# A Fourier tower's mixing written out with three buffers, and its inverse with half input tiles and two group buffers

## The reference, cut to what matters

```python
def _spectral_conv(h, w1, w2):
    xf = jnp.fft.rfft2(h)
    top = jnp.einsum('bixy,ioxy->boxy', xf[:, :, :M1, :M2], w1)
    bot = jnp.einsum('bixy,ioxy->boxy', xf[:, :, -M1:, :M2], w2)
    ...
    return jnp.fft.irfft2(of, s=(h.shape[-2], h.shape[-1]))
for l in range(LAYERS):
    sc = _spectral_conv(h, w1r[l] + 1j * w1i[l], w2r[l] + 1j * w2i[l])
    pw = jnp.einsum('bihw,oi->bohw', h, pw_w[l]) + pw_b[l][None, :, None, None]
    y = sc + pw
    ...
    h = jax.nn.gelu(y, approximate=False)
```

## Time and profile before

| | us |
|---|---|
| median of 3 runs | 5555.8 (5553.83 to 5564.04) |
| the profiled execution | 5561.11 |
| its span, first to last instruction | 5559.3 |

### The profile page before, as it was taken

How to read it: one execution, slowest core, us unless ns; L and a number is a source line. 1 busy time by engine, 2 the same in 40 slices (tenths; PEclk the granted TensorE clock), 3 DMA queues, 4 the chain that set the end, 5 groups by cost and what they waited for, 6 DMA issues and landing times. The chain is left out here.

```text
span 5559.3 us, 115640 instructions
## 1 busy us (share of the span) xinstructions
PE 3813.1 (69%) x50724; PEld 2545.1 (46%) x50724; DVE 2993.7 (54%) x3933; ACT 2535.4 (46%) x1968; POOL 56.9 (1%) x51
## 2 busy tenths in 40 slices
PE   5676885657666656576667566766678994668677
PEld 4354773435455534354555344545552223623532
DVE  1437987853666678536666784366660003344344
ACT  0112335521677755116777451167778991112122
POOL 0000000000000000000000000000000001000000
PEclk9888997888888878888889788888899995579579
DMA  1654656755677667556776675567765431000000
GB/s 34 253 215 172 224 219 258 288 213 226 243 288 289 268 253 289 219 211 257 289 289 257 264 281 224 207 257 288 288 258 206 170 123 36 0 0 1 0 0 8
DMA packets 184510, 1093.16 MB, mean 197 GB/s; under 512 B 20613, under 2 KB 92517, under 8 KB 122465
## 3 DMA queue, kind: packets, MB, share of 16 engines
q1 hardware_dynamic: 160578, 802.32, 37.6%
q10 hardware_dynamic: 22592, 285.22, 13.3%
q0 software_dynamic: 1024, 1.05, 0.1%
HBM read 683.80 MB, written 404.75 MB: 196 GB/s over the span
## 5 line engine op out<-in xcount | busy, mean ns | idle before, releaser
L509 PE MATMUL bank<-arena 128*64 128x128 f32 x16384 | 1130.4, 295 | 161.2 <-ACT arena L552 142.4
L509 PEld LDWEIGHTS bank<-arena 128*64 128x64 f32 x16384 | 1080.0, 221 | 314.0 <-issue 313.9
L587 DVE STREAM_TRANSPOSE arena<-bank 64x512 f32<-64x512 f32 x1024 | 731.4, 714 | 388.2 <-PE bank L485 357.3
L552 ACT ACTIVATE arena<-bank,pwb 128x1024 f32<-128x1024 f32 x512 | 567.0, 1108 | 608.0 <-PE bank L509 603.8
L543 ACT ACTIVATE arena<-arena,shift,scale 64x2048 f32<-64x2048 f32 x384 | 803.0, 2091 | 71.1 <-ACT arena L552 39.4
L361 PE MATMUL bank<-arena 128*32 128x128 f32 x8192 | 596.0, 476 | 309.0 <-DVE arena L388 309.0
L595 DVE BATCH_NORM_STATS2 stats<-arena 128x6 f32<-128x512 f32 x1024 | 634.0, 672 | 228.3 <-ACT arena L552 228.2
L361 PEld LDWEIGHTS bank<-arena 128*32 128x32 f32 x8192 | 423.4, 142 | 481.5 <-issue 327.6
L485 PE MATMUL bank<-arena,ga 64*64 64x512 f32 x2048 | 309.5, 728 | 476.2 <-DMA arena<-spec_out 420.8
L728 ACT ACTIVATE arena<-arena,shift,scale 128x1024 f32<-128x1024 f32 x384 | 445.1, 1230 | 404.5 <-DMA arena<-y_dram 404.3
L688 PE MATMUL bank<-arena,fwq 32*32 32x512 f32 x6144 | 316.9, 842 | 350.5 <-DVE arena L733 350.5
(11 more groups left out here) (208 smaller groups left out, 2845.5 us busy)
## 6 DMA issues: line engine op xcount, KB each, us to landing
arena<-y_dram SPq DMA_DIRECT2D x224, 2048.0 KB, 8.5
y_dram<-arena ACTq DMA_DIRECT2D x128, 2048.0 KB, 8.0
arena<-spec_in SPq DMA_DIRECT2D x32, 2048.0 KB, 8.9
arena<-in_w_modes SPq DMA_DIRECT2D x32, 2048.0 KB, 13.3
spec_out<-arena SPq DMA_DIRECT2D x64, 1024.0 KB, 3.9
arena<-spec_out SPq DMA_DIRECT2D x32, 2048.0 KB, 21.0
spec_in<-arena SPq DMA_DIRECT2D x24, 2048.0 KB, 13.4
spec_in<-arena ACTq DMA_DIRECT2D x4, 4096.0 KB, 11.7
```

The costliest lines, as they stand in the source:

```text
L509: mm = pe.matmul(hpx(bank[4 + T % 2 * 2 + j // 4][CHAN[par], :])[:, :, j % 4 * S:(j % 4 + 1) * S], a2[p % 2][par][:, :, rp], hpx(hin[u][pa ...
L552: act.activation(y, banks[:, 4 + T % 2 * 2:6 + T % 2 * 2, :].rearrange("p b (h x) -> p b h x", h=2), ACT.Identity, bias=pwb[:]).then_inc(y ...
L587: dve.transpose(a2[p % 2][par][FREQ[par], v * 32 + c0:v * 32 + c0 + 16, :], banks[FREQ[par], 2 * v:2 * v + 2, :].rearrange("p r (k c) -> p ...
```

## The change

Mixing: weights and spectra have three buffers in place of two, with semaphores of their own; the loops over chunks are written out. SP issues three chunks' loads, then the layer's small loads, then for each chunk the load of chunk c+3 (after the matmuls of chunk c) and behind it the store of chunk c. VectorE rotates chunk c+1 before it transposes chunk c. TensorE no longer waits for its own matmuls; `mix_done` takes the place of `mix_free`.

Inverse: `yin` is one pair's input in two halves of 1 MB, each loaded by itself once the two GELUs on it are done. `grp` has two buffers, and group g+1 is loaded in the first pair of group g, behind that pair's input. In layer 0 `load_x` is as before, with semaphores of its own.

```diff
-        w_loaded = [sem("w_loaded_even"), sem("w_loaded_odd")]
-        s_loaded = [sem("s_loaded_even"), sem("s_loaded_odd")]
+        w_loaded = [sem(f"w_loaded{u}") for u in range(3)]
+        s_loaded = [sem(f"s_loaded{u}") for u in range(3)]
...
-        mix_free, mixed_stored = sem("mix_free"), [sem("mixed_stored_even"), sem("mixed_stored_odd")]
-        w_sb = [at(u * MC * C, MC, C) for u in range(2)]
-        s_sb = [at(2 * MC * C + 2 * u * B * MC, 2, B, MC) for u in range(2)]
+        mixed_stored = [sem("mixed_stored_even"), sem("mixed_stored_odd")]
         HB = C // 2
-        m_sb = [[at(2 * MC * C + 4 * B * MC + (2 * u + v) * B * HB, B, HB) for v in range(2)] for u in range(2)]
-        IT = NCH // 2
+        w_sb = [at(u * MC * C, MC, C) for u in range(3)]
+        s_sb = [at(3 * MC * C + 2 * u * B * MC, 2, B, MC) for u in range(3)]
+        m_sb = [[at(3 * MC * C + 6 * B * MC + (2 * u + v) * B * HB, B, HB) for v in range(2)] for u in range(2)]
+        USES = [len(range(u, NCH, 3)) for u in range(3)]
+
+        def third(l, c):
+
+            return l * (USES[c % 3] * 16) + (c // 3 * 16 + 16)
...
         def sync_mix(sp, l, first):
-            def load(u, i2):
-
-                sp.wait_ge(mix_free, l * NCH + (i2 + (u + 1)))
-                sp.dma_start(s_sb[u][:, 0], spec_in[i2 + u]).then_inc(s_loaded[u], 16)
-                sp.dma_start(w_sb[u], d["w_modes"][l, i2 + u]).then_inc(w_loaded[u], 16)
-
-            def store(u, i2):
-                n = l * NCH + i2
+            def load(c):
+                u = c % 3
+                if c > 2:
+                    sp.wait_ge(mix_done, (l * NCH + c) * 2 - 4)
+                sp.dma_start(s_sb[u][:, 0], spec_in[c]).then_inc(s_loaded[u], 16)
+                sp.dma_start(w_sb[u], d["w_modes"][l, c]).then_inc(w_loaded[u], 16)
+
+            def store(c):
                 for v in range(2):
-                    sp.wait_ge(mixed_turned, n * 8 + (8 * u + 4 * v + 12))
-                    sp.dma_start(spec_out[2 * i2 + (2 * u + v)], m_sb[u][v].rearrange("p b o -> p (b o)")).then_inc(mixed_stored[u], 16)
-
-            for u in range(2):
-                load(u, 0)
-            with sp.Fori(0, IT - 1) as i:
-                for u in range(2):
-                    store(u, i * 2)
-                    load(u, i * 2 + 2)
-            for u in range(2):
-                store(u, (IT - 1) * 2)
-
+                    sp.wait_ge(mixed_turned, (l * NCH + c) * 8 + (4 * v + 12))
+                    sp.dma_start(spec_out[2 * c + v], m_sb[c % 2][v].rearrange("p b o -> p (b o)")).then_inc(mixed_stored[c % 2], 16)
+
+            for c in range(3):
+                load(c)
...
+            for c in range(NCH):
+                if c + 3 < NCH:
+                    load(c + 3)
+                store(c)
...
-            if first:
-                pe.sem_inc(mix_free, 2)
-            with pe.Fori(0, IT) as i:
-                for u in range(2):
-                    n = l * NCH + i * 2
-                    pe.wait_ge(w_loaded[u], (l * IT + i) * 16 + 16)
-                    pe.wait_ge(real_down, n + (u + 1))
-                    pe.wait_ge(imag_up, n + (u + 1))
-                    pe.wait_ge(imag_negated, n + (u + 1))
-                    for v in range(2):
-                        pe.wait_ge(mixed_turned, n * 8 + (8 * u + 4 * v + 4))
-                        pe.sem_inc(waited[pe.engine], 1)
-
...
-                        mm.then_inc(mix_done, 1)
-                    pe.wait_ge(mix_done, n * 2 + (2 * u + 2))
-                    pe.sem_inc(mix_free, 1)
+            for c in range(NCH):
+                u, n = c % 3, l * NCH + c
+                pe.wait_ge(w_loaded[u], third(l, c))
+                pe.wait_ge(real_down, n + 1)
+                pe.wait_ge(imag_up, n + 1)
+                pe.wait_ge(imag_negated, n + 1)
+                for v in range(2):
+                    pe.wait_ge(mixed_turned, n * 8 + (4 * v + 4))
+                    pe.sem_inc(waited[pe.engine], 1)
...
+                    mm.then_inc(mix_done, 1)
...
-            with dve.Fori(0, IT) as i:
-                for u in range(2):
-                    n = l * NCH + i * 2
-                    dve.wait_ge(s_loaded[u], (l * IT + i) * 16 + 16)
-                    dve.sem_inc(waited[dve.engine], 1)
-                    dve.tensor_copy(s_sb[u][C:P, 1], s_sb[u][0:C, 0]).then_inc(real_down, 1)
-                    dve.wait_ge(imag_up, n + (u + 1))
-                    dve.tensor_scalar(s_sb[u][C:P, 0], s_sb[u][C:P, 0], -1.0, None, ALU.mult).then_inc(imag_negated, 1)
-                    dve.wait_ge(mixed_stored[u], (l * IT + i) * 32 + 32)
-                    for v in range(2):
-                        dve.wait_ge(mix_done, n * 2 + (2 * u + v + 1))
-                        modes = banks[:, 4 * v:4 * v + 4, :].rearrange("p q (k r b) -> p b r (q k)", k=4, r=2)
-                        for j in range(4):
-                            dve.transpose(m_sb[u][v][:, 16 * j:16 * j + 16, :], modes[:, 16 * j:16 * j + 16]).then_inc(mixed_turned, 1)
...
-        grp_loaded, grp_free, pair_ready = sem("grp_loaded"), sem("grp_free"), sem("pair_ready")
-        in_loaded = [sem(f"in_loaded{u}") for u in range(2)]
+            def rotate(c):
+                u = c % 3
+                dve.wait_ge(s_loaded[u], third(l, c))
+                dve.sem_inc(waited[dve.engine], 1)
+                dve.tensor_copy(s_sb[u][C:P, 1], s_sb[u][0:C, 0]).then_inc(real_down, 1)
+                dve.wait_ge(imag_up, l * NCH + (c + 1))
+                dve.tensor_scalar(s_sb[u][C:P, 0], s_sb[u][C:P, 0], -1.0, None, ALU.mult).then_inc(imag_negated, 1)
+
+            rotate(0)
+            for c in range(NCH):
+                if c + 1 < NCH:
+                    rotate(c + 1)
+                dve.wait_ge(mixed_stored[c % 2], l * (NCH * 16) + (c // 2 * 32 + 32))
+                for v in range(2):
+                    dve.wait_ge(mix_done, (l * NCH + c) * 2 + (v + 1))
+                    modes = banks[:, 4 * v:4 * v + 4, :].rearrange("p q (k r b) -> p b r (q k)", k=4, r=2)
+                    for j in range(4):
+                        dve.transpose(m_sb[c % 2][v][:, 16 * j:16 * j + 16, :], modes[:, 16 * j:16 * j + 16]).then_inc(mixed_turned, 1)
+
...
+        grp_loaded, grp_free = [sem("grp_loaded_even"), sem("grp_loaded_odd")], sem("grp_free")
+        in_loaded = [sem("in_loaded_upper"), sem("in_loaded_lower")]
+        x_loaded = [sem("x_loaded_even"), sem("x_loaded_odd")]
...
-        yin = [at((6 + u) * PX, PX) for u in range(2)]
-        O1 = 8 * PX
-        grp = at(O1, M2, GI, HB)
-        O1 += C // 2 * GI * M2
+        yin = [at(6 * PX + v * PX // 2, 2, PX // 4) for v in range(2)]
+        O1 = 7 * PX
+        grp = [at(O1 + v * HB * GI * M2, M2, GI, HB) for v in range(2)]
+        O1 += C * GI * M2
...
+                for v in range(2):
+                    sp.sem_inc(in_loaded[v], NP * 16)
+
             def load_group(g):
-                sp.wait_ge(grp_free, l * NG + (g + 1))
-                sp.dma_start(grp.rearrange("p m b o -> p m (b o)"),
-                             spec_out[:, :, bass.ds(g * (GI * HB), GI * HB)].rearrange("m p x -> p m x")).then_inc(grp_loaded, 16)
-
-            def load_pair(p):
-                u, n = p % 2, l * NP + p
-                if first:
-                    if p > 1:
-                        sp.wait_ge(y_done, n * 4 + 4)
-                    for par in range(2):
-                        sp.dma_start(hin[u][par][C * par:C * par + 3, :],
-                                     d["x_pair"][p, 3 * par:3 * par + 3, :]).then_inc(in_loaded[u], 16)
-                else:
-                    if p > 1:
-                        sp.wait_ge(h_ready, n * 4 - 4)
-                    sp.dma_start(yin[u], y_dram[p]).then_inc(in_loaded[u], 16)
+                if g > 1:
+                    sp.wait_ge(grp_free, l * NG + g)
+                sp.dma_start(grp[g % 2].rearrange("p m b o -> p m (b o)"),
+                             spec_out[:, :, g * (GI * HB):(g + 1) * (GI * HB)].rearrange("m p x -> p m x")).then_inc(grp_loaded[g % 2], 16)
+
+            def load_half(p, v):
+                if p > 0:
+                    sp.wait_ge(h_ready, (l * NP + p) * 4 + (2 * v - 2))
+                px = slice(v * (ROW2 // 2), (v + 1) * (ROW2 // 2))
+                sp.dma_start(yin[v], hpx(y_dram[p])[:, :, px]).then_inc(in_loaded[v], 16)
+
+            def load_x(p):
+                if p > 1:
+                    sp.wait_ge(y_done, p * 4 + 4)
+                for par in range(2):
+                    sp.dma_start(hin[p % 2][par][C * par:C * par + 3, :],
+                                 d["x_pair"][p, 3 * par:3 * par + 3, :]).then_inc(x_loaded[p % 2], 16)
 
             load_group(0)
             if first:
                 sp.wait_ge(h_zeroed, 4)
             for p in range(NP):
-                if not first:
-                    load_pair(p)
-                if p % Q == 0 and p > 0:
-                    load_group(p // Q)
```

(36 more changed lines are left out.)

9 lines of the change are left out of this document (2 added, 7 removed).

## The result

The changed kernel takes 5234.0 us (5229.2 to 5239.7), against 5555.2 before: a ratio of 0.942 (0.940 to 0.944). That is 322 us less, clearly faster, but 149 short of the 471 forecast, and outside the range of 5000 to 5180.

The account below looks back on a forecast made before the run. It took waits as the bound, no engine being full, each stage with its own. 211 + 13 + 40 + 324 - 14 - 103 = 471 us off the 5555.8 median gave 5085, range 5000 to 5180.

Parts of the forecast that it names:

- Mixing, order on VectorE: Mixing: rotating chunk c+1 before transposing chunk c leaves TensorE no wait between chunks; gain 211 us, range 190 to 211.
- The branch: Mixing's loop over chunks: writing it out gains nothing counted; by the rows 0.02 us for each of 12 branches.
- Mixing, end: End of the mixing stage: small layer loads moved ahead of the stores shorten it to 4.3 us; gain 13 us.
- Inverse of layer 0: Two group buffers remove the wait for spectra at group boundaries; gain 40 us, down to 35.
- Inverse of layers 1 to 3: Removing group-load waits gains 324 us; late half tiles take back 14 in every pair and 103 at boundaries.
- Second half, every pair: Inverse of layers 1 to 3: second half tile lands barely in time, stalling 0.15 us a pair; 14 us, 0 to 48.
- One of the signs of being wrong: Inverse of layers 1 to 3: ScalarE waiting for y_dram a microsecond or more in each pair would refute the prediction.
- the choice at the boundary: First half behind a group load, layers 1 to 3: equal queue shares, stall 5.7 us, 18 times; 103 us, 0 to 142.
- Rival (c): Inverse of layers 1 to 3: single half tiles late in every pair by 1 to 2 us; 5215 us, chance 20%.
- The rule of packets: Second half beside the store: engines alternating queues by packet would land it a microsecond earlier, making 14 us 0; not adopted.

Follow-up runs that it names:

- the lone half: Kernel holding only loads, each waited for: the changed kernel's 1 MB pixel half, rows 16 KB apart; landed after 6.3 us.
- LEAD 5: Changed kernel with ScalarE's GELUs one step earlier ahead of the y outputs (5 in place of 4); 5293.9 us, ratio 0.953.
- the pitch: Changed kernel with the rows of y_dram 20 KB apart in place of 16 KB; 5185.4 us, ratio 0.933.
- the quarters: Changed kernel with the group load of layers 1 to 3 cut in four, one behind each pair's first half load; 5177.2 us, ratio 0.931.

## Why the prediction was wrong

*Mixing, order on VectorE: right.* No gap is left. 211 forecast, 219 measured (201.9 us a layer from the first matmul to the last became 147.1): eight chunks in one piece take 147.1 and not 149.0. The transfers fit, at a share of 0.77.

*The branch: small, as the rows had it.* The surplus of 8 us is that same 1.9 us a layer, four times. The Trainium skill, "Runtime: NRT & Kernel Launch", section "Instruction fetch mechanics", would put a stall at the taken branches on top of the 211. Whether those 1.9 us are the branches or the ends of the single chunks, no run separates.

*Mixing, end: right.* 4.6 us from the last transposes to the barrier (371.94 to 376.54) in place of 5.7 in layer 0. 13 forecast for all layers, about 15 measured.

*Inverse of layer 0: right.* 41 against 40.

*Inverse of layers 1 to 3: wrong, in one term above all.* The waits removed were as counted: none for spec_out but the first of each of these layers. The failed step is "Second half, every pair": "The remaining 0.92 MB of a half, at 381/0.91 = 419 GB/s, take 2.2 us". That put the half's landing 7.0 us after its issue, 2.2 after the store's. In the stretch shown three such halves landed after 9.6, 9.0 and 8.9 us, and 4.8, 3.3 and 2.9 after their stores. The term was 14 us, bounds 0 to 48; measured are 124, in 72 of the 96 pairs, 1.7 us each (the 18 pairs at a boundary and the first two of a layer have none). One of the signs of being wrong, a microsecond or more in each pair, came in most of them.

Two things in that step were off. The rate was the whole tile's, 16 KB in one piece, and two 4 KB pieces out of each 16 KB are slower: 6.3 us for the lone half, against 5.2 at another pitch. With the fast pitch 81 of the 124 us stay, so this is about a third. The rest is the half's place beside the store: with the half fast and asked for ahead of the store 24 us are left, with the latter alone 115. Why a fast half beside the store still takes 7.7 to 9.3 us stays open. The bound of 0.5 us a pair was too narrow because no row showed a load of this form.

The second term, the choice at the boundary, was mis-sized but not outside its range. "I take equal shares" gave 5.7 a boundary, 103 in all; measured are 7.0 on average, 126 in all, below the upper end of 7.9 and 142. The longest single wait was 8.1.

Together: GELUs wait 271 us for y_dram, of them 21 at the starts of the three stages, so 250 inside, where I counted 117. That is 133 of the 148 missing there. Of the other 15 some 9 are an estimate from the earlier trace rows: ScalarE's instructions overlap by 0.1 us (a y output at 1505.10 takes 1.11, the GELU behind it starts at 1506.11), and each of 90 waits loses that. The rest I did not trace.

Rival (c), late halves in every pair by 1 to 2 us, is what came, and had 20%. That its 5215 lies so near to 5234 is partly luck: 20 us less in the pairs than it said (124 for 144), 23 more at the boundaries, 15 outside both.

*The rule of packets.* The Trainium skill, "DMA: Bandwidth & Descriptors", "Queues, rings and completion order", would have shared the store's time from the start, and by it I had the half land a microsecond before my 7.0. It landed 1.9 to 2.6 us later than that 7.0, so neither reckoning gave the time. The store of 1362.00 landed after 7.3 us, as in the kernel before, those of 1377.29 and 1392.02 after 8.2 and 8.5; the runs don't tell sharing from waiting.

*Combinations.* LEAD 5, the pitch and the quarters gave -60, 49 and 57 alone and 170 together. Here the sums of single effects don't hold; that is shown. That LEAD 5 collides with the whole group load and needs fast halves is shown as well; how the queues bring it about is not.

## What to carry to other kernels

When a buffer is bought with another tile's room, price the smaller transfers by their exact shape: pieces, spacing and partitions, measured alone first. A half of a tile is half the bytes, not half the time. Then price it once more beside whatever the other queue moves at that moment. Where a large load shares a queue with small ones that are due, cut it and spread it, and judge an order of issues only after the transfers have the shape they will keep.

## What the runs showed of the hardware

- 1 MB read as two 4 KB pieces of each row lands after 6.3 us when rows are 16 KB apart, and after 4.9 to 5.5 at 18, 20, 24 and 32 KB. 8 KB of each 16 KB row: 5.1. Why 16 KB is slow is open.
- Beside a 2 MB store asked for 2.5 us earlier on the other queue, the same 1 MB lands after 7.7 to 9.3 us at 20 KB (5.0 ahead of the store) and after 8.9 to 9.6 at 16 KB (6.4).
- 1 MB into 64 partitions takes 7.2 us, nearly the 7.7 of 2 MB into 128.
- Straight code fed TensorE 2048 matmuls with their weight loads for 147 us without a gap, beside transfers at a share of 0.77.
